# The last FFN2 block of a quantized AdaLN + FFN kernel: seven quarter products for eight, with its own sums and rows

## What is computed

```python
def quant_linear(x, w, b):
    xq, s_in = quant_act_uint8(x)                 # one scale for the whole tensor
    wq, s_w = quant_weight_int8_perchannel(w)
    bq = quant_bias_int32(b, s_in, s_w)
    return jnp.einsum('btd,fd->btf', xq, wq) + bq
h = jax.nn.relu(quant_linear(x, w1, b1))          # w1 (2048, 512)
return quant_linear(h, w2, b2)                    # w2 (512, 2048)
...
x = x + _L0_ffn_ref(...)
```

## Time and profile before

| | us |
|---|---|
| median of three runs (lowest, highest) | 321.23 (320.97, 321.96) |
| time of the profiled execution | 321.04 |
| span of that execution | 319.2 |
| what lies around the span | 1.84 |

### The profile page before, as it was taken

How to read it: one execution, slowest core, us unless ns; L and a number is a source line. 1 busy time by engine, 2 the same in 40 slices (tenths; PEclk the granted TensorE clock), 3 DMA queues, 4 the chain that set the end, 5 groups by cost and what they waited for, 6 DMA issues and landing times.

```text
span 319.2 us, 4733 instructions
## 1 busy us (share of the span) xinstructions
PE 310.8 (97%) x1635; PEld 193.3 (61%) x1635; DVE 272.4 (85%) x602; ACT 200.7 (63%) x356; POOL 115.0 (36%) x96
## 2 busy tenths in 40 slices
PE   6999999999999999999999999999999999999995
PEld 6868888888776544444444444444458548647844
DVE  1699988997986699999999999999999698698855
ACT  2435775597386995466665664089959759677400
POOL 1066425634540599992180000710603301400410
PEclk9999999999999999999999999999999999999999
DMA  7999999999973379896990060060999996957952
GB/s 224 205 243 232 226 222 237 259 225 374 282 172 66 70 263 50 342 423 254 424 415 37 6 223 37 35 230 1 367 361 418 408 405 225 402 192 259 341 215 99
DMA packets 51624, 75.57 MB, mean 237 GB/s; under 512 B 20344, under 2 KB 34960, under 8 KB 46864
## 3 DMA queue, kind: packets, MB, share of 16 engines
q1 hardware_dynamic: 51408, 74.99, 78.2%
q10 hardware_dynamic: 192, 0.28, 0.5%
HBM read 45.89 MB, written 25.17 MB: 223 GB/s over the span
## 4 chain that ended last, share of the span: by engine, by line
PE 81%; DVE 11%; DMA 3%; issue 2%; SPq 2%; DVEq 0%
PE bank L589 24%; PE bank L714 21%; PE bank L816 15%; PE bank L826 11%; PE bank L686 6%; DMA x_in<-in_x_dram 3%; DVE hidden L1190 2%; PE bank L701 2%; DVE bank L1320 1%; DVE hidden L1051 1%; DVE bank L1315 1%; DVE hidden L1344 1%; DVE hidden L1342 1%; DVE hidden L1346 1%; DVE hidden L1347 1%
## 5 line engine op out<-in xcount | busy, mean ns | idle before, releaser
L816 PE MATMUL bank<-w_t 128*128 128x512 f16 (+1 forms) x272 | 55.9, 366 | 0.0
L1190 DVE TENSOR_SCALAR_CACHE_REDUCE hidden<-bank,qb,hmax 128x512 f32<-128x512 f32 x62 | 47.6, 806 | 6.4 <-PE bank L714 3.8
L494 POOL TENSOR_TENSOR x_lo<-hidden,x_hi 128x512 fp32r<-128x512 f32 x28 | 35.4, 1303 | 45.6 <-ACT x_hi L910 45.6
L589 PE MATMUL bank<-x_hi,cw_hi 128*128 128x512 f32 x128 | 48.4, 393 | 0.8 <-DVE hidden L1056 0.7
L589 PE MATMUL bank<-x_lo,cw_hi 128*128 128x512 f32 x128 | 48.4, 390 | 0.0
L589 PE MATMUL bank<-x_hi,cw_lo 128*128 128x512 f32 x128 | 48.4, 389 | 0.0
L570 POOL TENSOR_TENSOR pool_r<-pool_r,steps 128x512 f32<-128x512 f32 x16 | 20.2, 1274 | 75.3 <-DVE steps L1367 59.7
L1210 DVE CUSTOM_DVE_ANT_0 hidden<-hidden,bank,hmax 128x512 f32<-128x512 f32 x66 | 45.9, 743 | 0.2
L816 PEld LDWEIGHTS bank<-w_t 128*128 128x128 f16 x272 | 26.6, 98 | 28.3
L1016 ACT ACTIVATE pool_q<-hidden,s_quant 128x512 uint8<-128x512 f32 x63 | 39.1, 710 | 5.2 <-PE bank L826 4.9
L1016 ACT ACTIVATE w_t<-hidden,s_quant 128x512 uint8<-128x512 f32 x56 | 34.7, 709 | 11.7 <-PE bank L816 11.7
(11 more groups left out here) (157 smaller groups left out, 506.2 us busy)
## 6 DMA issues: line engine op xcount, KB each, us to landing
hidden_spill<-hidden SPq DMA_DIRECT2D x16, 1024.0 KB, 9.9
hidden<-hidden_spill SPq DMA_DIRECT2D x16, 1024.0 KB, 10.9
x_in<-in_x_dram SPq DMA_DIRECT2D x32, 256.0 KB, 7.1
pool_r<-in_x_dram SPq DMA_DIRECT2D x8, 1024.0 KB, 5.5
pool_q<-in_L_ffn_w_dram SPq DMA_DIRECT2D x7, 1024.0 KB, 10.2
out_dram<-pool_r SPq DMA_DIRECT2D x7, 1024.0 KB, 8.6
pool_r<-in_L_cond_W_dram SPq DMA_DIRECT2D x2, 1024.0 KB, 9.9
x_in<-in_L_ffn_w_dram SPq DMA_DIRECT2D x1, 1024.0 KB, 5.4
```

Of the source, the lines that this page charges most:

```text
L494: pool.tensor_tensor(x_lo[:, n % 2, k, :], x_t[:, k, :], x_hi[:, n % 2, k, :].bitcast(F32), ALU.subtract).then_inc(lo_ready, 1)
L589: return pe.matmul(REL[ot][:, :], w[:, k, ot * P:(ot + 1) * P], v[:, n % 2, k, :], start=(k == 0 and w is cw_hi and v is x_hi), stop=(k == ...
L816: return pe.matmul(y_bank[:, cols], hid_q[n % 2][:, ft, j * P:(j + 1) * P], w2_t[:, ft, cols], start=(ft == 0), stop=(ft == FT - 1))
L1190: dve.tensor_scalar(hidden[:, at:at + TB], y_bank[:, :], qb1[:, ft:ft + 1], hmax[:, ft:ft + 1], ALU.add, ALU.max, accum_out=hmax[:, ft:ft ...
```

## The change

1. Block 7 becomes a folded block, as `FOLDED = (2, 4, 6, 7)`. The special loops for the last block go away on PE and DVE.
2. Blocks 6 and 7 are now folded one behind the other, so block 7 has its own place for the sums (`HS[1]`, in slot 1 of `hidden`) and for the rows (`OUT_ROWS[1]`, at that slot's end). Its hidden values are therefore reloaded to slot 2, and may be reloaded only when block 5 has been rounded; SP issues that reload behind the store of block 2 and the load that reuses its place.
3. In all folded blocks the keeping of partial results is split. DVE adds the bias to the bank in place (`bias`, 4 times a block: b1a, b1b, b5a, b5b), and then ACT copies six partial results to SBUF (`keep`), between its rounding of the next block's tiles. DVE's takes fall from 22 to 18. PE waits for `fold_kept` (ACT) where it waited for DVE's keeps.
4. The bias on the fifth product's bank is `b2_over`, the difference of the two halves of the bias, made by one more DVE instruction of 256 columns when the constants are made.
5. The order of the 14 part products changes: "1a", "1b", "2a" now lead, and "5b" comes straight behind "7a".
6. DVE makes the first half of block 7's sums within block 6, between the take of "5b" and that of "4a", and behind it, and the second half at the start of block 7. POOL's row additions of block 6 wait for these.
7. Of block 7, rows 0 and 2 are added to x by POOL and stored whole; rows 1 and 3 are finished by DVE in four pieces of 256 columns.

```diff
-        FOLDED = (2, 4, 6)
+        FOLDED = (2, 4, 6, 7)
-        SLOT = (0, 1, 2, 3, 1, 2, 3, 1)
+        SLOT = (0, 1, 2, 3, 1, 2, 3, 2)
-        PRODUCTS = ("1a", "5a", "6a", "3a", "7a", "2a", "1b", "4a", "5b", "6b", "3b", "7b", "2b", "4b")
+        PRODUCTS = ("1a", "1b", "2a", "5a", "6a", "3a", "7a", "5b", "4a", "6b", "3b", "7b", "2b", "4b")
+        KEEPS = ("k1a", "k1b", "k5a", "kxa", "k5b", "kxb")
+        TAKES = ("b1a", "b1b", "c11a", "m11a", "b5a", "c12a", "m12a", "c22a", "m22a", "b5b", "m21a", "c12b", "m12b",
+                 "c22b", "m22b", "c11b", "m11b", "m21b")
+        LAST_PIECES = [("m12b", 1, LAST), ("m22b", 3, LAST), ("m11b", 1, FIRST), ("m21b", 3, FIRST)]
...
-                    sp.wait_ge(hid_ready, tiles_to({5: 3, 6: 4, 7: 5}[n]))
+                    sp.wait_ge(hid_ready, tiles_to({5: 3, 6: 4, 7: 6}[n]))
...
             store(1)
             reuse(1)
-            reload(SLOTS + 3)
             store(2)
             reuse(2)
+            reload(SLOTS + 3)
             store(3)
             reuse(3)
...
@@ PE, folded(n)
                 part2(0, a11, B11, F1[0], start=True)
+                part2(1, a11, B11, F1[1], start=True)
+                part2(0, a12, B21, F2[0], start=True)
                 pe.wait_ge(hs_ready, sums + 5)
-                part2(0, HS[0], W2S[0], F5, start=True)
-                pe.wait_ge(fold_taken, takes_to(n, "k1a"))
+                part2(0, hs[0], W2S[0], F5, start=True)
+                pe.wait_ge(fold_kept, keeps_to(n, "k1a"))
                 pe.wait_ge(hs_ready, sums + 6)
+                part2(0, hs[1], W2S[1], F1[0])
+                pe.wait_ge(fold_kept, keeps_to(n, "k5a"))
                 pe.wait_ge(hs_ready, sums + 7)
+                part2(0, hs[3], B22, F5)
+                pe.wait_ge(fold_kept, keeps_to(n, "kxa"))
                 pe.wait_ge(hs_ready, sums + 8)
+                part2(0, hs[2], W2S[2], F1[0])
+                pe.wait_ge(fold_taken, takes_to(n, "m12a"))
+                part2(1, hs[0], W2S[0], F5, start=True)
                 pe.wait_ge(fold_taken, takes_to(n, "c22a"))
                 part2(0, a22, W2S[3], F1[0])
...
                 pe.wait_ge(fold_taken, takes_to(n, "c22b"))
                 part2(1, a22, W2S[3], F1[1])
...
@@ ACT
+            def keep(n, name, product, row, cols, r):
+                if product[0] == "6":
+                    act.wait_ge(fold_done, products_to(n, product))
+                else:
+                    act.wait_ge(fold_taken, takes_to(n, "b" + product))
+                act.activation(OUT_ROWS[n % 2][:, row, cols], r[:, FIRST], ACT.Copy).then_inc(fold_kept, 1)
+
+            def keeps(n, rounded):
+                if rounded == 2:
...
+                    keep(n, "k1a", "1a", 0, FIRST, F1[0])
+                elif rounded == 4:
+                    keep(n, "k1b", "1b", 1, FIRST, F1[1])
+                elif rounded == 5:
+                    keep(n, "k5a", "5a", 2, LAST, F5)
+                    keep(n, "kxa", "6a", 0, LAST, F1[0])
+                elif rounded == 9:
+                    keep(n, "k5b", "5b", 3, LAST, F5)
+                elif rounded == 11:
+                    keep(n, "kxb", "6b", 1, LAST, F1[1])
...
@@ DVE
+            dve.tensor_tensor(b2_over, b2_b[:, LAST], b2_b[:, FIRST], ALU.subtract).then_inc(consts_ready, 1)
...
             def finish_folded(n):
+                plain = n - 1 in PLAIN
+                if not plain:
+                    sums12(n, 1)
+                bias(n, "1a", F1[0], b2_b[:, FIRST])
+                if not plain:
+                    sums43(n, 1)
+                elif two:
                     add_bias(n - 1, 2)
+                bias(n, "1b", F1[1], b2_b[:, FIRST])
                 if two:
                     scale_y(n - 1, 2)
+                    add_x(n - 1, 2)
+                elif plain:
                     add_bias(n - 1, 3)
+                result(n, "c11a", "2a", 0, FIRST, F2[0], F2[0], "k1a")
+                bias(n, "5a", F5, b2_over)
                 if two:
                     add_bias(n - 1, 3)
+                elif plain:
                     scale_y(n - 1, 3)
+                result(n, "c12a", "3a", 0, LAST, F5, F5, "kxa")
+                result(n, "c22a", "7a", 2, LAST, F1[0], FV, "k5a")
+                bias(n, "5b", F5, b2_over)
                 if two:
                     scale_y(n - 1, 3)
+                if plain:
                     add_x(n - 1, 3)
+                if n + 1 in FOLDED:
+                    sums12(n + 1, 0)
+                dve.wait_ge(fold_done, products_to(n, "4a"))
+                scale_row(n, 2, FIRST, F1[0])
+                if n + 1 in FOLDED:
+                    sums43(n + 1, 0)
+                result(n, "c12b", "3b", 1, LAST, F5, F5, "kxb")
+                result(n, "c22b", "7b", 3, LAST, F1[1], FV, "k5b")
+                result(n, "c11b", "2b", 1, FIRST, F2[1], F2[1], "k1b")
+                dve.wait_ge(fold_done, products_to(n, "4b"))
+                scale_row(n, 3, FIRST, F1[1])
```

More of the change, by code:

```diff
@@ L293, in adaln_quantized_ffn @@
         ROWS = {n: (0, 2, 1, 3) if n in FOLDED else (0, 1, 2, 3) for n in BY_POOL}
+        ROWS[NB - 1] = (0, 2)
         FIRST = slice(0, HALF)
         LAST = slice(HALF, TB)
-        F1, F5, F2, FV = (bank[0], bank[3]), bank[1], bank[2], bank[7]
-        PRODUCTS = ("1a", "5a", "6a", "3a", "7a", "2a", "1b", "4a", "5b", "6b", "3b", "7b", "2b", "4b")
-        TAKES = ("k1a", "k5a", "kxa", "c12a", "m12a", "c22a", "m22a", "c11a", "m11a", "k1b", "c21a", "m21a", "k5b",
-                 "kxb", "c12b", "m12b", "c22b", "m22b", "c11b", "m11b", "c21b", "m21b")
@@ L304, in adaln_quantized_ffn, with rows_to @@
-        ROW_TAKES = ("m11a", "m21a", "m11b", "m21b")
+        F1, F2, F5, FV = (bank[0], bank[3]), (bank[2], bank[5]), bank[1], bank[7]
+        ROWS_OWNER = {n: max([m for m in BY_POOL if m < n and m % 2 == n % 2], default=None) for n in FOLDED}
+        def rows_to(n, row=None):
+            return sum(len(ROWS[m]) for m in BY_POOL[:BY_POOL.index(n)]) + (ROWS[n].index(row) + 1 if row is not None else 0)
+        PRODUCTS = ("1a", "1b", "2a", "5a", "6a", "3a", "7a", "5b", "4a", "6b", "3b", "7b", "2b", "4b")
@@ L861, in folded @@
-                pe.wait_ge(fold_taken, takes_to(n, "m11a"))
-                part2(1, a12, B21, F2, start=True)
+                pe.wait_ge(fold_kept, keeps_to(n, "k1b"))
+                part2(1, hs[1], W2S[1], F1[1])
+                pe.wait_ge(fold_kept, keeps_to(n, "k5b"))
+                part2(1, hs[3], B22, F5)
+                pe.wait_ge(fold_kept, keeps_to(n, "kxb"))
+                part2(1, hs[2], W2S[2], F1[1])
+                if n - 1 in PLAIN:
+                    pe.wait_ge(y_taken, plain_to(n - 1, 2))
@@ L863, in folded @@
+                part2(1, a12, B21, F2[1], start=True)
                 pe.wait_ge(fold_taken, takes_to(n, "c22b"))
@@ L875, in _ @@
                         mm.then_inc(y_done, 1)
-            for n in range(1, NB - 1):
+            for n in range(1, NB):
                 if n in FOLDED:
@@ L1018, in _ @@
                                    ACT.Copy, scale=s_quant[:, ft:ft + 1]).then_inc(hid_ready, 1)
+                    if n - 1 in FOLDED:
+                        keeps(n - 1, i + 1)
+            for i in range(FT):
+                keeps(NB - 1, i + 1)
         @block.vector
@@ L1346, in sum_hidden, with bias, result @@
                 dve.tensor_tensor(t4, a12, t2, ALU.subtract).then_inc(hs_ready, 1)
                 dve.tensor_tensor(t3, a21, a11, ALU.subtract).then_inc(hs_ready, 1)
+            def bias(n, product, r, units):
+                dve.wait_ge(fold_done, products_to(n, product))
+                dve.tensor_tensor(r[:, FIRST], r[:, FIRST], units, ALU.add).then_inc(fold_taken, 1)
+            def result(n, name, product, row, cols, r, to, kept):
+                dve.wait_ge(fold_done, products_to(n, product))
+                dve.wait_ge(fold_kept, keeps_to(n, kept))
+                dve.tensor_tensor(to[:, FIRST], OUT_ROWS[n % 2][:, row, cols], r[:, FIRST], ALU.add
+                                  ).then_inc(fold_taken, 1)
+                dve.wait_ge(fold_taken, takes_to(n, name))
+                scale_row(n, row, cols, to)
@@ new lines, in scale_row @@
+            def scale_row(n, row, cols, r):
+                if n == NB - 1 and row not in ROWS[n]:
+                    at = (SLOTS - 1) * WC + row * D + cols.start
+                    xs = x_res[:, at:at + HALF]
+                    dve.tensor_tensor(r[:, FIRST], r[:, FIRST], s2_b[:, cols], ALU.mult).then_inc(fold_taken, 1)
+                    name = [m for m, j, c in LAST_PIECES if (j, c) == (row, cols)][0]
+                    dve.wait_ge(fold_taken, takes_to(n, name))
+                    dve.wait_ge(xres_landed[1], 16 * SLOTS)
+                    dve.tensor_tensor(xs, xs, r[:, FIRST], ALU.add).then_inc(last_added, 1)
+                    return
+                dve.tensor_tensor(OUT_ROWS[n % 2][:, row, cols], r[:, FIRST], s2_b[:, cols], ALU.mult
```

(23 more changed lines are left out.)

147 lines of the change are left out of this document (64 added, 83 removed).

## The result

| | us |
|---|---|
| before, median of 4 runs | 321.1 (320.95 to 321.96) |
| changed kernel, median of 4 runs | 329.12 (326.74 to 329.89) |
| ratio, 95% interval | 1.0233 (1.0183 to 1.0283) |
| forecast, range | 325.2, 323.2 to 327.7 |
| profiled execution of the changed kernel, its span | 329.78, 328.0 |

The direction was right and the size was not: +8.0 us against +4.0. The median lies outside the range. Rival 1, the late reload of block 7, came true, and it cost more than its 2.6 us.

What follows compares the result with a forecast made beforehand. PE was taken to bound the kernel, busy 97% of the span. A saving of 1.60 us and other terms, mostly added waits, summed to +3.94 on 321.04, giving 324.98, and 0.19 for the median: 325.2 us, range 323.2 to 327.7.

Steps and rivals of the forecast that it cites:

- Rival 1: Block 7's reload, issued only after ACT rounds block 5, lands late and delays block 7: +2.6, 327.8 us; chance 0.18.
- tail, behind the end of issue: After block 7: DVE's last add ends 2.02 us behind PE's end of issue, before 1.59: +0.43.
- its forecast 0.17: Block 2: the extra bias operation in DVE's queue moves DVE's first take from 1.14 to 1.31 us after block start.
- 3a's stall: Block 2: product "3a" waits for DVE's bias on "5a" and ACT's copy, starting at 5.70 instead of 4.37: +1.33 us.
- seven for eight: Block 7, now folded, needs less PE time, falling from 13.82 to 12.22 us: -1.60.
- the likeliest case: Whole kernel: the forecast of 324.2 to 326.2 us, chance 0.52.
- at no price: Items put at no cost: POOL's rows, DVE's four fewer takes, SP's shorter pieces, and reloading block 7 later.
- the threshold: Block 7's reload: block 7 is delayed if the reload takes over 14.1 us.
- rival 2: ScalarE's copies cost little or the waits overlap better: up to 2.0 us less, 323.2; chance 0.16.
- Rivals 3 and 4: Folded blocks: added stalls don't arise, 319.5 us, chance 0.06; or only 0.24 and 0.25 a block stay, 321.4, chance 0.08.
- Rival 3: Folded blocks: results, copies and hops take 0.25 us less together, so added stalls don't arise: 319.5 us; chance 0.06.

Runs made afterwards that it cites:

- The kernel with the reload in time: Changed kernel with block 7's reload issued by quarters, ahead of the load reusing block 2's place: 325.13 us; with only reload and that load swapped on SP: 324.91.
- reordered kernels: Changed kernel with reload by quarters and PE, DVE and ACT orders rewritten per folded block: 320.54 us; then also the last six stores reordered: 319.45.
- the run with PE kept at work: Changed kernel, reload as it is, plus 2 x 6 unread matmuls of 512 columns on PE in block 6 ahead of waits for ACT's copies: 327.04 us.
- the last kernel: Changed kernel with reload by quarters and all orders rewritten, then only the order of the last six stores on SP changed: 319.45 us.

## Why the prediction was right and where it was wrong

**Right: the terms of the sum.** The kernel with the reload in time shows them undisturbed. In us, a block from its start on PE to the start of the next:

| step | forecast | measured |
|---|---|---|
| block 2, whole | 13.83 | 13.64 |
| block 4, whole | 13.06 | 13.05 |
| block 6, whole | 13.94 | 13.98 |
| block 7, whole | 13.76 | 13.79 |
| tail, behind the end of issue | 2.02 | 2.06 |
| copy of 256 columns on ACT | 0.39, next after 0.30 | 0.38, next after 0.28 |

The 13.05 of block 4 is the same in the changed kernel. Block 7's 13.79 runs from 305.37 to the end of issue of the product that starts at 318.29. The one term that was off is `b2_over`: DVE's first take in block 2 came at 237.86, no later than before, so its forecast 0.17 was nothing, and 3a's stall there was 1.12 and not 1.33. The sum came out at 325.2 against 325.13 and 324.91 measured, and no large errors hide in it: none of the blocks is off by over 0.2.

**Right: why seven for eight brings nothing by itself.** PE's 1.60 us were saved, and the waits gave back more. The reordered kernels show that this was the order's doing. Their folded blocks of 12.2 us have the same instructions on all engines.

**Wrong: the likeliest case had the reload in time.** The step that failed is the last item of "at no price", reloading block 7 later, and the figures of rival 1. Put at nothing in the sum, the late reload cost 4.0 us by the medians (329.12 less 325.13). Three things were mis-sized.

1. *The issue.* I put it at 277.9, when ACT has rounded block 5. I had moved the reload behind `reuse(2)` in my list and not priced the wait that stands there. That wait is for the store of block 2, which lands 9.9 us behind its own issue. The issue of the reload came at 279.05, 1.4 later than ACT allowed. In the run with PE kept at work the same store landed at 277.21, and the wait cost nothing: this part depends on the execution.
2. *The move.* I took 14.1 us as the threshold and held 10.2 us of pure transfer against it. The earlier trace rows already had 16.7 from first issue to last landing, with a load ahead and a store behind. The same two neighbours stand beside it in the new order, and it took 15.5. Bytes and rate were both off: in those 15.5 us (279.05 to 294.54) the core moved 5.5 MB and not 4.2, as its neighbours moved with it, at 358 GB/s and not 412. With the load ahead gone the reload took 12.4.
3. *The consequence.* I passed the lateness on to block 7 alone: 16.7 would cost 2.6. The copies of block 6 stand behind block 7's tiles in ACT's queue, so PE lost the time in block 6, in two gaps of 1.57 and 1.33 us, 2.7 us net, and then ran at half its clock, another 2.2 us. The 2.7 is close to rival 1's 2.6 by luck: the rival had it in block 7, from an earlier issue and a longer move. The clock's cost stood in none of the cases, and it takes the time past rival 1's 327.8.

Even with the issue at 277.9 the rival had 13.6 to 14.1 us of room, against the 16.7 of the earlier trace rows. By the rows it was the likeliest case, not one of 0.18.

**Rivals 2 to 4.** The copies cost what was taken, so rival 2 falls. Rivals 3 and 4 needed PE to find its banks free at once or nearly so; it didn't in this order. Rival 3's figure, 319.5, is what the last kernel reaches, by the order of things and not by shorter terms.

## What to carry to other kernels

Work for an earlier stage that is put into an engine's queue between instructions for a later one inherits every wait of the later one: ask of each inserted instruction what the instruction ahead of it waits for, DMAs included. When a transfer is moved behind another on an issuing queue, price the wait in front of the other first, and take its duration from the row with the same neighbours, not from its own bytes over the rate of a full stretch. When an engine is full, count the time between a product and the next one in the same bank and set the order of all engines by it. The same instructions, stores included, gave 325.1 us in one order and 319.5 in another; which of the many moves are needed was not tried one by one.

## What the runs showed of the chip

**PE's clock fell without a long stop.** No gap of PE in block 6 exceeded 1.6 us. The stretches of the changed kernel (clock third from the end):

```profile
294.00:296.30 2.30, 0.73 (x8) 0.42 (x6) 0.02 (x1) 1.68 (x4) 0.00 (x0) 1.00 1.03 396
296.30:298.65 2.35, 1.02 (x9) 0.68 (x9) 1.79 (x4) 2.35 (x6) 0.00 (x0) 0.78 0.10 32
298.65:300.30 1.65, 1.65 (x8) 1.18 (x9) 0.00 (x0) 1.65 (x4) 0.00 (x0) 0.50 0.22 38
300.30:303.70 3.40, 3.40 (x18) 2.42 (x16) 1.71 (x4) 1.01 (x2) 0.00 (x0) 0.50 0.89 256
```

PE was busy for 1.75 of the 4.65 us from 294.00 to 298.65, and the granted clock was then 0.50, the 1.2 GHz level, until past 303.7, although PE worked again without a stop. Single shorter gaps, 0.96 in block 2 and 0.91 in block 7, left it at 1.00. That the gaps brought the fall is read from this order of events; no run shows the same gaps with the clock held.

**A store of 1 MB landed 9.9 us after its issue** (268.77 to 278.63) with a 1 MB load issued 0.4 us ahead of it. The core moved 216 GB/s in that time, 2.1 MB, which is about the load and the store; at the 409 GB/s of block 2's stretch they would take 5.1 us (an estimate). So its bytes and the load ahead do not explain its time. What it waited for was not tried.
